# A three-stage decoder kernel: the third stage's unit inputs as high and low parts for two tiles at once, its context keys and values made in the second stage, unrolled turns, new orders

## The reference

```python
x = x + L0_attn(layernorm(x))                    # gated linear attention, first stage
x = x + L0_wkv(layernorm(x), ctx)                # recurrence over the context, second stage
x = x + L0_experts(layernorm(x))                 # 8 experts, top 2, second stage
x = x + L1_attn(layernorm(x))                    # D: 16 heads, 4 key heads, rope, sink
x = x + L1_xattn(layernorm(x), ctx, ctx)         # E
x = x + L1_ffn(x)                                # F: attention that modulates; M: the units
# E, per token: heads attend to heads
Q = (q @ Wq.T + bq).reshape(bs, sl, 16, 16)
K = (k @ Wk.T + bk).reshape(bs, sl, 16, 16)
V = (v @ Wv.T + bv).reshape(bs, sl, 16, 16)
score = einsum('bshd,bsgd->bshg', Q, K)
attn = einsum('bshg,bsgd->bshd', softmax(score), V).reshape(bs, sl, 256)
return attn @ Wo.T + bo
# M: 1024 units
gate_pre = h @ W_in_base.T + mod * (h @ A) @ B
mlp_out = silu(gate_pre) * (h @ W_up_base.T) @ W_down.T
```

## Time and profile before

| | |
|---|---|
| Median of 3 runs | 3676.59 us (3674.57 to 3690.04) |
| Profiled execution | 3677.66 us, span 3675.7 us |
| Busy | PE 85%, DVE 70%, POOL 57%, ACT 49% |
| Granted TensorE clock, mean | 0.921 |
| First stage | 0 to about 1540 us |
| Second stage | about 1540 to 2153 us, the recurrence until about 1900 |
| Third stage | about 2153 us to the end |

### The profile page before, as it was taken

How to read it: one execution, slowest core, us unless ns; L and a number is a source line. 1 busy time by engine, 2 the same in 40 slices (tenths; PEclk the granted TensorE clock), 3 DMA queues, 4 the chain that set the end, 5 groups by cost and what they waited for, 6 DMA issues and landing times. The chain is left out here.

```text
span 3675.7 us, 71094 instructions
## 1 busy us (share of the span) xinstructions
PE 3132.7 (85%) x22664; PEld 2495.4 (68%) x22696; DVE 2581.5 (70%) x5658; ACT 1789.9 (49%) x3717; POOL 2096.5 (57%) x2554
## 2 busy tenths in 40 slices
PE   6789999999999999755289955788888888888888
PEld 3668888888888888644244433566766666666667
DVE  6668888888888888666433325677777777777762
ACT  5667877777877778522123322333333333333321
POOL 5666666666666666577400016666666666666660
PEclk8989999999999999977599976899999999999999
DMA  3445444444444444311111130000000000000000
GB/s 125 138 146 159 137 142 150 132 142 131 146 128 148 136 142 136 132 53 40 55 61 63 63 109 14 8 12 12 14 12 14 11 11 11 11 11 11 7 8 6
DMA packets 173790, 274.90 MB, mean 75 GB/s; under 512 B 41207, under 2 KB 107127, under 8 KB 172938
## 3 DMA queue, kind: packets, MB, share of 16 engines
q1 hardware_dynamic: 167436, 255.39, 21.6%
q0 software_dynamic: 6144, 16.79, 1.4%
HBM read 218.31 MB, written 45.39 MB: 72 GB/s over the span
## 5 line engine op out<-in xcount | busy, mean ns | idle before, releaser
L1608 POOL TENSOR_TENSOR l_prod<-l_sco,l_vE 128x256 f32<-128x256 f32 x512 | 414.8, 851 | 251.3 <-DVE l_sco L2108 251.3
L1600 POOL TENSOR_TENSOR l_prod<-l_q,l_kv 128x256 f32<-128x256 f32 x512 | 367.4, 754 | 121.2 <-DVE l_att L2116 121.2
L717 DVE SCALAR_TENSOR_TENSOR a_cq<-a_PQ,a_taps,a_cq 128x504 f32<-128x504 f32 (+2 forms) x384 | 281.8, 734 | 129.7 <-ACT a_cq L583 120.6
L717 DVE SCALAR_TENSOR_TENSOR a_ck<-a_PK,a_taps,a_ck 128x504 f32<-128x504 f32 (+2 forms) x384 | 280.8, 731 | 11.0 <-ACT a_ck L583 1.9
L341 POOL TENSOR_TENSOR a_tq<-a_cq,a_tq 128x512 f32<-128x512 f32 x128 | 165.7, 1294 | 153.6 <-ACT a_tq L589 153.6
L411 PE MATMUL a_PQ<-a_x_hi,a_wqk 128*128 (+1 forms) x512 | 202.4, 436 | 52.2 <-POOL a_wqk L292 39.1
L328 POOL TENSOR_TENSOR a_hrs<-a_hve,a_neghalf 128x8 f32<-128x8 f32 x128 | 209.4, 1636 | 22.9 <-DVE a_hve L734 22.9
L484 PE MATMUL a_Y<-a_wo,a_og_parts 128*128 128x256 f32 x1536 | 206.1, 284 | 9.4 <-POOL a_og_parts L335 9.4
L411 PEld LDWEIGHTS a_X<-a_wv,a_xb 128*128 128x128 f32 x1536 | 199.9, 188 | 12.1 <-issue 1.2
L411 PE MATMUL a_X<-a_wv,a_xb 128*128 128x256 f32 x1536 | 204.1, 282 | 0.8 <-DMA a_xb<-a_x_lo 0.8
L484 PEld LDWEIGHTS a_Y<-a_wo,a_og_parts 128*128 128x128 f32 x1536 | 194.5, 192 | 11.2 <-issue 10.2
(11 more groups left out here) (374 smaller groups left out, 8840.5 us busy)
## 6 DMA issues: line engine op xcount, KB each, us to landing
a_wqk<-qk_parts SPq DMA_DIRECT2D x112, 512.0 KB, 3.3
a_wv<-v_parts SPq DMA_DIRECT2D x56, 512.0 KB, 3.8
a_wg<-g_parts SPq DMA_DIRECT2D x112, 256.0 KB, 3.3
a_wo<-o_parts SPq DMA_DIRECT2D x112, 256.0 KB, 2.9
a_dr<-decays SPq DMA_DIRECT2D x256, 64.0 KB, 2.5
m_hs<-sorted_rows SPq DMA_DIRECT2D x72, 128.0 KB, 2.1
sorted_outs<-m_ys SPq DMA_DIRECT2D x72, 128.0 KB, 1.7
qk_parts<-a_wqk SPq DMA_DIRECT2D x16, 512.0 KB, 3.3
```

The costliest lines, as they stand in the source:

```text
L717: nc.vector.scalar_tensor_tensor(out=acc, in0=src, scalar=taps[p][:, tap + k:tap + k + 1], in1=acc, op0=ALU.mult, op1=ALU.add).then_inc(s_ ...
L1600: nc.gpsimd.tensor_tensor(out=prod[:, h], in0=qv[:, h:h + 1, :].to_broadcast([P, H, HD]), in1=kk, op=ALU.mult).then_inc(S("E_pqk"), 1)
L1608: nc.gpsimd.tensor_tensor(out=prod[:, h], in0=sco[:, h:h + 1, :].to_broadcast([P, HD, H]), in1=vv, op=ALU.mult).then_inc(S("E_pav"), 1)
```

## The change

Only the second and third stages are touched.

- **Keys and values.** `recurrence_and_experts` now makes the context's keys and values of all 32 tiles: after `k_T`, PE runs `cross_kv` for two tiles (per tile a bias product of three bfloat16 rows and two float32 products, 128x512, into halves of the PSUM tile TV), and for two more after `ranks`; ACT copies each out (`kv_out`), SP stores it to DRAM. `v_T` now waits for the last of these copies. `layer_one` loads the result into three buffers; `e_cT`, both `e_kv` and `et_keep` are gone.
- **Biases** of the query and of the output come by a three-row bfloat16 product in PE (`biased`); the additions on DVE are gone, and ACT copies the query out.
- **Normalise** of D and E moves from DVE to ACT, with a small product on POOL (`nm`) and a small negation on DVE (`ng`).
- **Units.** `win`, `wup`, the unit input and the modulation are split into high and low float32r parts. `m_half` makes two units for two tiles at once, 256 columns wide, by three products per weight block (high x high, high x low, low x high), and the modulation by one product of 96 rows. Splitting costs ACT `f_x2hi`, `ft_gm_hi`, DVE `f_x2lo`, `ft_gm_lo` per tile, and at the start `split_high` and `split_low` on all the weights.
- **Single copies.** `xT` is no longer doubled: `f_v` and `d_v` are one product each instead of two; ACT moves the values out in four pieces instead of two.
- **Turns** are all written out. M starts a turn later, the projection (Md) two turns later than before. All five lists are reordered.

```diff
-    FIRST = dict(G=-2, Dn=-1, D=0, Dt=1, En=1, E=2, Et=3, F=4, Ft=5, M=6)
+    FIRST = dict(G=-2, Dn=-1, D=0, Dt=1, En=1, E=2, Et=3, F=4, Ft=5, M=7, Md=8)
...
+                def cross_kv(b, tiles):
+
+                    pe.wait_ge(S("vt"), b + 1)
+                    if b == 0:
+                        pe.wait_ge(S("kv_w"), 32)
+                    for j in tiles:
+                        if j >= 2:
+                            pe.wait_ge(S("kv"), BT * b + j - 1)
+                        nc.tensor.matmul(TV[:, j % 2, :], ones3[:], bkv[:], start=True, stop=False)
+                        for c in range(DC):
+                            at = c * (NS // DC) + 2 * j
+                            last = nc.tensor.matmul(TV[:, j % 2, :], vt[:, at:at + 2, :], wkv[:, c, :], start=False, stop=c == DC - 1)
+                        last.then_inc(S("kvp"), 1)
...
                     if f is not None:
                         k_T(f)
+                        cross_kv(f, (0, 1))
                     if r is not None:
                         h_T(r)
                         router(r)
                         ranks(r)
+                    if f is not None:
+                        cross_kv(f, (2, 3))
...
+            PASSES = [(c, i, j) for c in range(DC) for i, j in ((0, 0), (0, 1), (1, 0))]
+
             def m_half(half):
...
+                    for name, w, bank, done in (("GA", win, GA, "M_g"), ("UA", wup, UA, "M_u")):
+                        free(name, f"m_{half}", t)
+                        for k in range(2):
...
+                            for c, i, j in PASSES:
+                                last = nc.tensor.matmul(out, w[:, i, c, units], x2[pair % 2][:, j, c, :], start=(c, i, j) == PASSES[0],
...
+                            if name == "GA":
+                                last = nc.tensor.matmul(out, fb3[:, units], gm3[pair % 2][:], start=False, stop=True)
...
-            iterate(pe, [("M", m_half(0)), ("D", d_xT), ("Dt", d_eT), ("E", e_xT), ("D", d_qk), ("Dt", d_av), ("F", f_zT),
-                         ("E", e_cT), ("Ft", ft_eT), ("E", e_q), ("Ft", ft_av), ("E", e_kv), ("F", f_qk), ("D", d_qkT), ("Dt", d_oT),
-                         ("M", m_half(1)), ("Dt", d_wo), ("F", f_v), ("Ft", ft_oT), ("D", d_v), ("D", d_s),
-                         ("Ft", ft_a), ("M", m_down), ("Et", et_aT), ("Et", et_wo), ("F", f_s)])
+            iterate(pe, [("M", m_half(0)), ("E", e_xT), ("D", d_xT), ("Dt", d_eT), ("D", d_qk), ("Dt", d_av), ("Ft", ft_eT), ("E", e_q),
+                         ("M", m_half(1)), ("Dt", d_oT), ("F", f_zT), ("Dt", d_wo), ("Ft", ft_av), ("D", d_qkT), ("D", d_v), ("F", f_qk),
+                         ("Ft", ft_oT), ("D", d_s), ("Ft", ft_a), ("Md", m_down), ("Et", et_aT), ("Et", et_wo), ("F", f_s), ("F", f_v)])
```

More of the change, by code:

```diff
@@ L1647, in product, with biased @@
                 return last
+            def biased(out, bias, lhsT, rhs):
+                nc.tensor.matmul(out, ones3[:], bias[:], start=True, stop=False)
+                for c in range(DC):
+                    last = nc.tensor.matmul(out, lhsT(c), rhs(c), start=False, stop=c == DC - 1)
+                return last
             def turn(bank, src):
@@ L1708, in d_v @@
                 free("EB", "d_v", t)
-                for s in range(2):
-                    last = product(EB[:, s * 64:(s + 1) * 64], lambda c: twice("D", c, s), lambda c: dwv[:, c, :])
-                last.then_inc(S("D_pv"), 1)
+                product(EB[:, 0:64], lambda c: xT["D"][:, c, :], lambda c: dwv[:, c, :]).then_inc(S("D_pv"), 1)
             def d_s(t):
+                pe.wait_ge(S("D_q"), t + 1)
                 pe.wait_ge(S("D_kx"), KX * (t + 1))
@@ L1784, in f_v @@
                 free("P1", "f_v", t)
-                for s in range(2):
-                    last = product(P1[:, s * D:(s + 1) * D], lambda c: twice("F", c, s), lambda c: fwv[:, c, :])
-                last.then_inc(S("F_pv"), 1)
+                product(P1[:, 0:D], lambda c: xT["F"][:, c, :], lambda c: fwv[:, c, :]).then_inc(S("F_pv"), 1)
             def f_s(t):
+                pe.wait_ge(S("F_qk"), t + 1)
                 pe.wait_ge(S("F_kx"), KX * (t + 1))
```

369 lines of the change are left out of this document (204 added, 165 removed).

## The result

The changed kernel takes 3396.9 us in the median (3393.2 to 3402.0), the kernel before 3675.6 on the same chip: ratio 0.922, 95% interval 0.920 to 0.925. The gain is 279 us; 177 were forecast, and the range ended 8 us above the result. The profiled execution took 3393.2 with a span of 3391.5.

A forecast was written before the change was run, and what follows sets the result against it. No engine was full; the third stage's turn was a loop PE, VectorE, GpSimd. Own time 3677.7 - 214 (turns) + 36 (second stage) + 5 (start) - 5 (end) = 3499.7, forecast 3499 us; 8 in 10: 3405 to 3595.

The forecast's parts named there:

- the six instructions: Third stage, VectorE: F's two norms, residual add, two rope sums, new low part meet value products; 0.44 each, 2.6 us.
- I take 1.8 us for both: Third-stage turn: VectorE waits for PE's late units' second half and for D's late `divide` inputs; 1.8 us, between 0 and 4.
- 31.6 + 2.6 = 34.2: Third-stage turn: VectorE's work end to end after removals and additions, 31.6, plus 2.6 collision surcharge, comes to 34.2 us.
- VectorE runs undisturbed: Rival, third stage: no surcharge and no wait on VectorE, turn 33.2, gain 301, time 3412 us; chance 0.22.
- The estimate of 2.3 us on average: Third stage: by the skill's rule each of six VectorE instructions waits up to one GpSimd product; 2.3 us on average.
- its worst case of 4.6: Third stage: at worst the rule's waits for products cost VectorE 4.6 us a turn, 62 us more over 31 turns.
- 6 x 4.4 = 26: Second stage: two tiles' keys and values ahead of the router, 2.2 us each, lengthen six steps; 26 us lost.
- costing them at nothing: Second stage: the two tiles behind the ranks hide behind GpSimd's scatter of over 10 us; cost nothing.
- 10 us for both: Second stage, first two steps: no scatter to hide behind, four tiles' products delay the next transposes; 10 us lost.
- where 5 were to be lost: Start: the weights' split stands ahead of the third stage's first scores; about 5 us lost, between 0 and 20.
- forecast 5: End: two more but short turns, as the units' products halve; 5 us gained, between 10 lost and 15 gained.
- K: Theory from the experiments, third stage: value products 13.9, last value sum's end 1.5, VectorE's list to the weights 17.7; no slack.

The follow-up runs named there:

- combine in the gap: Changed kernel with VectorE's full-width combine moved right ahead of the weights, where GpSimd forms no products, second pair of row buffers: 3406.8 us, turn 33.8.
- combine of one column: Changed kernel with the combine made for one of its 256 columns, in its old place ahead of the weights: 3386.0 us, turn 32.9.
- combine in the window: Changed kernel with VectorE's combine moved behind `d_x`, where GpSimd forms value products, second pair of row buffers: 3407.3 us, turn 33.7.
- small products: Changed kernel with GpSimd's query-key and weight-value products made for one sixteenth of their elements, VectorE's sums at full size: 3302.5 us, turn 30.3.

## Why the prediction was right or wrong

**Right.** Faster; that TensorE leaves the bound; that GpSimd's waits are where the gain is; that what is put beside the value products takes longer: four of the six instructions over twice their time, one half as much again, the low part hardly. The surcharges of the five, start to start against the kernel before, are 0.20, 0.53, 0.56, 0.56 and 0.64 us, 2.5 in all, where 2.6 stood in the sum for six. Unit products at 0.13 to 0.16 a record.

**Wrong: the turn, 36.0 against 33.2 us, 87 us of the miss.** Two steps failed.

- *"I take 1.8 us for both"*, the waits on TensorE. They were 0 in the pictured turn and 0.2 in the mean. I had reckoned that TensorE would stand idle for 4 us ahead of the units' second half. Its list has `d_eT`, `d_qk`, `d_av`, `ft_eT` and `e_q` there, and in the pictured turn no idle piece of it is longer than 1.13 us, with 1.01 ahead of `e_q` and 0.35 ahead of the units' second half; the clock stayed at 1.00. The cost exists: with the combine in the gap TensorE came back at 0.50 in most turns and its scores of F were late by 0.8 us. In the changed kernel TensorE comes back low in some turns, and VectorE hardly waits for it.
- *"31.6 + 2.6 = 34.2"*, VectorE's list end to end. It is 33.0. I priced what newly collides and forgot what stops colliding when the lists shift: L2115 0.85 to 0.29 us, the combine 1.96 to 1.50, together 1.0 less. The statistics, which no longer have waits among them, take 0.5 less. About 0.5 more lies in instructions that a wait used to part and that now overlap their predecessor by 0.08 us. Against that the low part of the modulation collides (0.85 us, where 0.6 stood for it and two negations), and so does L2110 (+0.3). And what left VectorE's list had taken 3.3 us of it start to start, not 3.5: I had added durations, which overlap by 0.08 us.

**Right number, wrong mechanism.** The rival "VectorE runs undisturbed" had a turn of exactly 33.2. But VectorE is not undisturbed: its collisions are 4.2 us a turn. The number was reached because other terms of the sum were smaller, and that is luck for this rival.

**The rule of the Trainium skill** (SBUF — State Buffer, Who interferes with whom: such instructions lock each other out for a whole instruction) agrees with these runs: the combine of one column still takes 0.50 us, and a product that meets `f_x2lo` takes 1.00 in place of 0.81. The estimate of 2.3 us on average was near the 2.5 measured; its worst case of 4.6 did not occur.

**The second stage, 36 against 28.4 us (641.4 - 613.0), with its split upside down.** *"6 x 4.4 = 26"* was 9.6 up to the last router. The price was right: in a step the two tiles in front of the router take 4.4 us and stand on the path. The step that failed is that all else on the path was left as it was. GpSimd's scatter takes 9.9 us in place of 12.2: before, two of its eight instructions took 2.30 and 1.91 us, each beside one of VectorE's scans of 2.3 us, and now all take 0.96 to 1.06, with no scan beside them. From `h_T` to the scatter it is 0.4 us less, and `k_T` takes 7.2 us (clock 1.00) or 8.8 (0.81) where it took 8.05 (0.78). That gives the steps of 31.5 and 33.1 us in place of 30.7. The two tiles behind the ranks fill what had been TensorE's longest wait, 10.3 us ahead of `k_T`, now 2.4 to 2.9: costing them at nothing was right. *"10 us for both"* first steps was 18.3: in the sum no step asked what the new stores queue behind. They lie behind 6 MB of expert weights, and ScalarE, with two buffers, stood 10.8 us for one.

**Start and end.** The third stage's start gained some 6 us where 5 were to be lost (the ends of that estimate were 0 and 20: below nothing was left out for no reason), and no run shows why; the end gained 7 (forecast 5).

What bounds the turn now is shown in part. The four pieces of K, as means over 29 turns of each profile:

| us | value products | to the last sum | last sum | chain |
|---|---|---|---|---|
| changed | 13.85 | 0.47 | 1.20 | 17.82 |
| norms of F and rope ahead of the weights | 13.03 | 1.73 | 1.21 | 20.42 |
| norms of F on ScalarE | 13.51 | 0.76 | 1.20 | 17.97 |
| combine in the window | 14.03 | 2.00 | 1.21 | 16.62 |
| the same, and norms on ScalarE | 13.93 | 1.42 | 1.20 | 17.19 |
| combine of one column | 13.82 | 0.58 | 1.20 | 17.41 |
| the same, and norms on ScalarE | 13.64 | 1.15 | 1.20 | 17.13 |
| combine in the gap | 13.81 | 0.70 | 1.20 | 18.19 |

The chain gets longer and shorter as the edits say. What is taken out of it comes back in the second column, in part with one column and wholly in the other runs, where the last sum comes late behind `f_x2lo` or behind the window's other work. So K names the right pieces, and it is shown that relieving the window alone gives nothing. The only gain from a shorter chain is that of one column, 0.34 us; whether moving `f_x2lo` would give more stays open. Beside the loop stand, within a microsecond, the window's own work and TensorE's scores of F, and GpSimd works 29.4 of 33.2. Which would come next if the chain alone became shorter by over a microsecond was not tried without moving collisions at the same time.

## What to carry to other kernels

When two engines both touch SBUF, price a reordering by who meets whom on both sides: what starts to collide, and what stops. A small instruction that meets a long product can cost mostly the wait for that product, so shrinking it saves little (merging small ones might save more; no run here tried it). A collision can still be the cheaper choice, when the same instruction would otherwise stand on the chain that another engine waits for. When an engine looks full, take work off it in two different places before believing that its total is the bound. When you price an insertion, ask also what else on the path moves out of a collision by it.

## What the hardware showed that was not expected

- Of VectorE's instructions beside GpSimd's products only some are held up. Adds and scalings of SBUF tiles are (0.42 to 0.98, one column 0.50); sums over 1024 elements (1.21 a piece), instructions with a PSUM operand (L2207 0.68) and the statistics' single-element operations (0.15) are the same with small products as with full ones.
- GpSimd pays too: 13.9 us for 16 value products where VectorE holds more such instructions beside them, 13.0 before.
- Moving work to an undisturbed place made the kernel slower: the two instructions took 0.4 us less, but TensorE, from standing for its bank, came back at a granted clock of 0.50 in 19 of 26 turns, where it does so in 8 of 27 of the changed kernel.
- GpSimd's scatter meets VectorE's scans as well: 2.30 and 1.91 us for an instruction that takes 0.96 with none beside it.
